# A vision-transformer tower on one core: the small steps of each image rebuilt and put in other places of the attention loop

## The reference

```python
emb = jnp.einsum('bnk,ek->bne', patches, W) + b            # embed
h = emb + pos_embed
...
q = (x @ Wq + bq).reshape(B, N, H, hd)                     # x = _layernorm(h)
k = (x @ Wk + bk).reshape(B, N, H, hd)
v = (x @ Wv + bv).reshape(B, N, H, hd)
scores = jnp.einsum('bihd,bjhd->bhij', q, k) / jnp.sqrt(jnp.asarray(hd, x.dtype))
...
attn = jax.nn.softmax(scores + col_bias[None, :, None, :], axis=-1)
out = jnp.einsum('bhij,bjhd->bihd', attn, v).reshape(B, N, D)
h = h + (out @ Wo + bo)
...
logits = tokens.astype(jnp.float32) @ router_w.astype(jnp.float32).T   # tokens = _layernorm(h)
combine = jnp.zeros((N, E), tokens.dtype).at[jnp.arange(N)[:, None], re].set(rw)
for e in range(E):
    g = jax.nn.gelu(tokens @ w1[e] + b1[e], approximate=False)
    out = out + combine[:, e:e + 1] * (g @ w2[e] + b2[e])
```

## Time and profile before

| | |
|---|---|
| median of 3 executions | 1240.35 us (1239.73 to 1240.62) |
| profiled execution, its own time | 1236.63 us |
| its span, first to last instruction | 1234.4 us |
| PE busy | 1131.5 us (92%) |
| ACT busy | 1034.6 us (84%) |
| DVE busy | 737.2 us (60%) |
| POOL busy | 117.8 us (10%) |
| start, until the first exponential | 73.7 us |
| attention, first to last exponential | from 73.70 to 1071.66 us |
| granted PE clock, each of 40 slices | 9 tenths or more (mean 1.000) |

### The profile page before, as it was taken

One profiled execution on the slowest core, in us unless ns is written; L12 is line 12 of the kernel. 1 busy time (PEld: TensorE's weight loads), 2 busy tenths in 40 slices (PEclk: granted clock), 3 DMA queues, 4 the chain that ended last, 5 costly groups with the idle time before them and its releaser, 6 DMA issues. The chain is left out here.

```text
span 1234.4 us, 23587 instructions
## 1 busy us (share of the span) xinstructions
PE 1131.5 (92%) x8738; PEld 343.7 (28%) x8738; DVE 737.2 (60%) x1953; ACT 1034.6 (84%) x1124; POOL 117.8 (10%) x128
## 2 busy tenths in 40 slices
PE   2269999999999999999999999999999999899998
PEld 2022222222222222222222222222222222243332
DVE  8734365656565656565657575757565641567654
ACT  0059999999999999999999999999999999945553
POOL 4303010101010101000101000000000100000000
PEclk9999999999999999999999999999999999999999
DMA  1133131323131313131313132222222230022231
GB/s 39 53 79 82 37 84 45 81 49 81 49 80 50 80 50 80 49 80 50 80 51 79 50 77 53 68 55 77 59 66 57 58 85 4 14 64 69 65 85 48
DMA packets 61672, 75.96 MB, mean 62 GB/s; under 512 B 25988, under 2 KB 31108, under 8 KB 61532
## 3 DMA queue, kind: packets, MB, share of 16 engines
q1 hardware_dynamic: 59452, 73.78, 23.3%
q10 hardware_dynamic: 1600, 0.27, 0.1%
q0 software_dynamic: 480, 0.06, 0.1%
HBM read 37.47 MB, written 36.49 MB: 60 GB/s over the span
## 5 line engine op out<-in xcount | busy, mean ns | idle before, releaser
L1126 ACT ACTIVATE probs<-psum 128x1024 f32<-128x1024 f32 x1024 | 951.2, 1106 | 46.1 <-PE psum L1319 45.4
L1335 PE MATMUL psum<-probs,VA 128*32 128x512 f32 x4096 | 545.6, 605 | 8.2 <-DVE oT L1194 7.4
L1319 PE MATMUL psum<-QA,KA 54*128 54x512 bf16 x2048 | 349.4, 386 | 34.0 <-ACTq L1145 10.3
L1319 PEld LDWEIGHTS psum<-QA,KA 54*128 54x128 bf16 x2048 | 81.5, 93 | 535.7 <-ACT probs L1126 493.2
L1335 PEld LDWEIGHTS psum<-probs,VA 128*32 128x32 f32 x4096 | 82.6, 108 | 139.2 <-issue 105.1
L1194 DVE STREAM_TRANSPOSE oT<-psum 128x512 f32<-128x512 f32 x64 | 45.8, 715 | 122.9 <-PE psum L1335 122.2
L1161 ACT ACTIVATE probs<-psum,b 128x1024 f32<-128x1024 f32 x64 | 67.8, 1110 | 54.3 <-PE psum L1388 54.2
L1266 DVE TENSOR_TENSOR probs<-probs,psum 128x1024 f32<-128x1024 f32 x64 | 78.1, 1221 | 51.6 <-PE psum L1398 32.5
L1126 ACT ACT_TABLE_LOAD x1 | 1.3, 1283 | 72.4 <-issue 72.4
L1388 PE MATMUL psum<-m_x,w 64*128 64x512 f32 x256 | 60.5, 591 | 1.5 <-ACT probs L1161 1.5
L1412 PE MATMUL psum<-probs,w 128*64 128x512 f32 x256 | 60.9, 598 | 0.0
(11 more groups left out here) (182 smaller groups left out, 936.8 us busy)
## 6 DMA issues: line engine op xcount, KB each, us to landing
QA<-q_parts_d SPq DMA_DIRECT2D x64, 192.0 KB
KA<-k_parts_d SPq DMA_DIRECT2D x64, 192.0 KB
q_parts_d<-qk_parts SPq DMA_DIRECT2D x32, 192.0 KB, 2.5
k_parts_d<-qk_parts SPq DMA_DIRECT2D x32, 192.0 KB, 2.7
xT<-in_xT SPq DMA_DIRECT2D x16, 256.0 KB, 3.4
q_parts_d<-qk_parts SPq DMA_DIRECT2D x32, 128.0 KB, 2.7
k_parts_d<-qk_parts SPq DMA_DIRECT2D x32, 128.0 KB, 2.5
x_d<-x2T SPq DMA_DIRECT2D x16, 256.0 KB, 2.0
```

Source lines behind the costliest of these rows:

```text
L1126: nc.scalar.activation(probs[:, k % PROB_BUFS, :], score_buf(buf_of(k)), ACT.Exp).then_inc(exped, 1)
L1319: last = pe.matmul(score_buf(buf_of(k))[:, (g % 2) * BANK:(g % 2 + 1) * BANK], KA[rows_of(h, SCORE_ROWS), h // 2, jt * P:(jt + 1) * P], QA ...
L1335: last = pe.matmul(o_acc[32 * g:32 * g + 32, :], VA[:, jt, h, :], probs[:, k % PROB_BUFS, (g % 2) * BANK:(g % 2 + 1) * BANK], start=(jt == ...
```

## The change

1. **Block-diagonal weights.** The weights of `embed`, `v` and `out_proj` are laid out as 128 x 128 with the 64 x 64 matrix twice on the diagonal. The tokens of an image's first and second half stand above each other on the partitions, so one matmul gives two chunks of tokens. Eight matmuls with 64 columns become four with 128.
2. **fp32 instead of three bf16 parts.** The normalised tokens are transposed in fp32 (`norm_t`, four transposes, as in `post_t`) and projected in fp32. `split_tokens`, `norm_t0` and `norm_t1`, the splitting of the weights on POOL at the start, and the three-turn matmuls go. `qk0` and `qk1` are each two fp32 matmuls with 64 rows and 256 columns.
3. **Halves.** `qk0`, `qk1`, `out_proj`, `router`, `v` and `embed` are each issued in two halves in two slots. With the five steps that stay whole there are 17 pieces. Only the second half raises `aux_filled`.
4. **Another order.** See the table in the diff. `qk1` instead of `v` is now followed by the splitting of q and k. `evacuate` now stands ahead of the slot's step in DVE's queue. `centre_tokens` moves from behind `out_proj` to slot 9 and `scale_tokens` to slot 10, both ahead of the read-out of `sq`. The ranking moves to slots 20 and 22, and the router's exponential on ACT from block 52 to block 39.
5. **Two images ahead.** `embed` and `norm_t` work for the image after the next. The start therefore embeds two images (`FIRST_STEPS`), and SP loads patches three images ahead.
6. **The output bias.** It was a row of `w_o` fed by a row of ones in `oT_norm`. Now POOL adds it to the residual once for each image (`add_bo`, 128 x 512 fp32), and DVE waits for that before `out_proj` is read out. Because of the new layout of `w_o` one second transposition of `evacuate` (`ON`) serves all, at slot 1, instead of two.

```diff
-AUX_SLOTS = {2: ["embed"], 7: ["norm_t0"], 8: ["norm_t1"], 9: ["qk0"], 10: ["qk1"], 11: ["v"], 14: ["sq"],
-             18: ["out_proj"], 19: ["flag"], 23: ["post_t"], 25: ["router"], 31: ["combine_t"]}
+AUX_SLOTS = {0: ("qk0", 0), 1: ("qk0", 1), 3: ("qk1", 0), 4: ("qk1", 1), 6: ("out_proj", 0), 7: ("out_proj", 1),
+             10: ("sq", 0), 13: ("post_t", 0), 15: ("flag", 0), 16: ("router", 0), 18: ("router", 1), 20: ("v", 0),
+             21: ("v", 1), 23: ("embed", 0), 24: ("embed", 1), 26: ("combine_t", 0), 29: ("norm_t", 0)}
+FIRST_STEPS = [("embed", 0), ("norm_t", 0), ("qk0", 0), ("qk1", 0), ("v", 0), ("embed", 1), ("norm_t", 1), ("sq", 0),
+               ("flag", 0)]
+CENTRE_SLOT, SCALE_SLOT, NORM_SLOT = 9, 10, 27
-COMBINE_SLOT = 26
+COMBINE_SLOT, WEIGH_SLOT = 20, 22
...
+            def add_bo(b):
+                g.wait_ge(xn_made, b + 1)
+                rows = H_all[:, ds(b * NCH, NCH), :]
+                g.tensor_tensor(rows, rows, b_o[:, :].unsqueeze(1).broadcast_to([P, NCH, D]),
+                                ALU.add).then_inc(bo_added, 1)
...
                 if step == "embed":
                     pe.wait_ge(x_loaded, 16 * (n + 1))
-                    for c in range(NCH):
-                        last = pe.matmul(aux[:, c * D:(c + 1) * D], xT[:, c * P:(c + 1) * P], w_tok[:, :],
+                    for c in chunks:
+                        last = pe.matmul(aux[:, c * P:(c + 1) * P], xT[:, c * P:(c + 1) * P],
+                                         w_tok[:, :, :].rearrange("k t e -> k (t e)"), start=True, stop=True)
...
+                elif step in ("qk0", "qk1"):
+                    rows = slice(D * int(step[-1]), D * int(step[-1]) + D)
+                    for i in halves:
+                        cols = slice(i * BANK // 2, (i + 1) * BANK // 2)
+                        last = pe.matmul(aux[:, cols], w_qk[rows, :, :].rearrange("k a e -> k (a e)"), xnT[rows, cols],
                                          start=True, stop=True)
...
+                def body(b):
+                    add_bo(b)
+                    if b:
+                        post_pow(b - 1)
...
+                        if slot == LAST_EVAC_SLOT and b:
+                            evacuate(b - 1, 3)
+                        if slot in EVAC_SLOTS:
+                            evacuate(b, EVAC_SLOTS[slot])
+                        if slot == CENTRE_SLOT and b:
+                            centre_tokens(b - 1, st)
+                        if slot == SCALE_SLOT and b:
+                            scale_tokens(b - 1, st)
+                        if slot == NORM_SLOT and b + 2 < NB:
+                            normalise(b + 2)
+                        found = step_of(b, slot)
+                        if found and is_last(found[0], found[1]):
```

More of the change, by code:

```diff
@@ L69, with step_of, is_last, aux_order @@
 TINY = 1e-30
-QK_COLS, V_COLS = slice(0, 2 * D), slice(2 * D, 3 * D)
-W_COLS = 3 * D
-TURNS = ((0, 0), (1, 0), (2, 1))
 SECOND = 64
 Q_ROWS = SECOND + H
-ONE_ROW = 31
 ds = bass.ds
 FB_UNITS = 4 * NCH
[L85 to L97, removed]
+def step_of(b, slot):
+    if slot not in AUX_SLOTS:
+        return None
+    step, part = AUX_SLOTS[slot]
+    image = b + (2 if step in LEAD else 1 if step in PREP else -1)
+    return (step, part, image) if 0 <= image < NB else None
+def is_last(step, part):
+    return part == 1 or step not in HALVED
+def aux_order(b):
+    found = [step_of(b, slot) for slot in range(QUADS)]
+    return [f[0] for f in found if f and is_last(f[0], f[1])]
+def aux_before(b):
+    return len(FIRST_STEPS) + sum(len(aux_order(i)) for i in range(b))
+def aux_count(b, step):
+    return aux_before(b) + aux_order(b).index(step) + 1
 def token_unit(b):
@@ L572, in tensor_steps, with aux_step @@
         def tensor_steps(pe):
-            def aux_step(step, n, done, drained):
-                pe.wait_ge(aux_drained, drained) if not (isinstance(drained, int) and drained == 0) else None
+            def aux_step(step, n, drained, part=None):
+                halves = (0, 1) if part is None else (part,)
+                chunks = [c for c in range(NCH // 2) if c // 2 in halves]
+                if drained and 0 in halves:
+                    pe.wait_ge(aux_drained, drained)
                 if step == "embed":
@@ L634, in aux_step @@
                                             ident_bf[:, :])
-                last.then_inc(aux_filled, 1)
+                if 1 in halves or step not in HALVED:
+                    last.then_inc(aux_filled, 1)
             return aux_step
@@ new lines, in _ @@
+                    link(v.memset(lower[:, :, :], 0.0))
+                    for e in range(1, NX):
+                        last = v.memset(lower[:, e, 0:e], 1.0)
+                    last.then_inc(const_ready, 1)
+                    v.wait_ge(w_loaded, 16 * WEIGHTS)
+                    for i, (step, n) in enumerate(FIRST_STEPS[1:7]):
+                        if step in LEAD:
+                            lead_step(step, n, i + 2)
+                        else:
+                            prep_step(step, n, i + 2, st)
+                        if step == "embed":
+                            normalise(n)
@@ L1145, in fallback, with body @@
                         act.sem_inc(fb_moved, FB_MOVED)
-                def body(b, first, last):
+                def body(b):
                     act.wait_ge(flag_ready, b + 1)
@@ L1153, in body @@
                         exp_block(b, k)
-                        if k == ROUTER_EXP_BLOCK and not first:
-                            router_exp(aux_base(b) + aux_order(not last, True).index("router") + 1)
+                        if k == ROUTER_EXP_BLOCK and b:
+                            router_exp(aux_count(b, "router"))
                 def gelu(u):
```

361 lines of the change are left out of this document (169 added, 192 removed).

## The result

The kernel after takes 1314.06 us (median of 5, 1307.64 to 1316.02) against 1240.35: 1.0586 of the time, 95% interval 1.0569 to 1.0603. It is slower, as forecast, but by 74 us and not by 35: outside the range of 1247 to 1298. The profiled execution took 1307.64 us (before: 1236.63), with a span of 1305.6 and a mean granted PE clock of 0.967 (before: 1.000).

The account below looks back on a forecast made before the run. ACT was taken as the bound, idle only when PE's scores come late. 1236.6 + 30 (attention) + 5 (start) - 0.9 (experts) + 1 (POOL) = 1271.7 profiled; with 3.7 to the median, 1275 us; range 1247 to 1298.

Parts of the forecast that it names:

- The bound: Attention, kernel before: ACT bounds, idle 2.8 us an image waiting for PE's scores; 58.8 us if PE were never late.
- the 0.78: Between scores and `values`: PE may be 0.78 us late before ACT loses any time.
- the ledger: PE's lateness per quad: falls 0.30, rises by step times and waits, excess over 0.78 lost; 6.05 us an image.
- Slots 13 to 16: PE waits for DVE's read-outs ahead of `post_t` and `flag`, then half of `router`: 3.15 us an image lost.
- Slots 0 to 4: Halves of `qk0` and `qk1`, with PE waiting for `oT` and `qk0`'s read-out: 1.45 us an image lost.
- Slot 26: `values` waits for `oT` behind DVE's normalisation of `embed`: 0.85 us an image lost.
- The pieces: PE time of new halves: 0.57 us for `embed`, `v`, `out_proj`, 0.54 for `qk`, 0.5 for `router`; all under 0.78.
- POOL's addition: `add_bo` at an image's start, some 2.3 us long: costs 0.1 us an image, +1 us in all.
- The rival with the shared port: `oT_norm` waits for `add_bo` to end, up to 1.5 us an image: 1297 us; chance 0.10.
- The start: Before the first exponential: 8.2 us of second `embed` on DVE less 3.0 saved, +5 us (bounds +3 and +7).
- The experts: Expert stretch: `out_proj` has half as many instructions, -0.9 us.
- the price of the wait ahead of `flag`: Slot 15: PE waits 2.3 us for `post_t`'s read-out, losing 1.85 us an image.

Follow-up runs that it names:

- d: kernel 1 with POOL's `add_bo` moved from the image's start to behind `prep_rstd`: 62.63 us an image against 63.02, 1237.22 us.
- b: kernel 1 with DVE reading `qk0` out ahead of `evacuate` in slot 1: 61.85 us an image against 63.02, 1227.12 us.
- experiment 6: The kernel after with all DVE and POOL reorderings, every step whole in its second half's slot: 1203.38 us, against 1200.08 with halves.
- kernel 1: The kernel after with DVE's work on `sq` that follows `excess` moved behind the read-out of `flag`: 1243.08 us, 63.02 us an image.
- kernel 1 with five additions: kernel 1 with five idle 512-column additions on DVE ahead of the read-out of `post_t`: 1303.29 us, 67.8 us an image.

## Why the prediction was right, and where it was wrong

- **The bound, the 0.78 and the ledger** held. Full-clock images took 64.98 against 64.8.
- **Slots 13 to 16** (3.15 forecast): waits of 1.21 and 2.12 against 1.2 to 1.4 and 2.3. Taken away they gave back 0.99 and 1.96.
- **Slots 0 to 4** (1.45): `qk1` waited 0.92, not 0.75. Without POOL's addition it waits 0.5 (d), so DVE's own chain was 0.25 shorter than forecast and the addition gave 0.4 of the wait. b gave back 1.17.
- **Slot 26** (0.85): 0.87.
- **The pieces**: a half 0.64 where I took 0.57, within the bounds; `qk` 0.52 where I took 0.54 (475.61 to 476.13). Little hangs on it, as experiment 6 shows.
- **POOL's addition**: 1.29 us long, not 2.3, and dearer than I took it: 0.39 an image, 6 us and not 1. The rival with the shared port had the place right, and about a quarter of its price of 1.5 us an image was measured.
- **The start**: +2.45, not +5. DVE was later at the bias by 59.64 - 54.42 = 5.2 us, as the working said, and the shift rows were as late. But before, their 24 KB went out at 65.53 and the load that waits for them was issued at 70.29 (4.8 us), behind the loads of the parts, issued from 62.42 to 65.4; after, it took from 70.70 to 72.74. That the loads ahead of them make the difference is read from the order alone. A wait ended last that the sum didn't look for: the transfers'.
- **The experts**: -1.0 against -0.9.

Profiled execution against profiled execution, the sum was 1271.7 and the time 1307.64, so 35.9 are missing, and the clock is 36. That these meet so well is partly luck: the start came 2.5 us cheaper than forecast, and the attention at full clock dearer (33 against 31 + 1 in thirteen images, +0.4 against -1.3 in the other three, the last of which had a fall too). **The step that failed is the price of the wait ahead of `flag`**, 1.85 us an image in the sum: "PE waits 2.3" was right, and the price was taken as if PE came back from the wait at the same speed. At full clock it was worth 1.96; the fall of the granted clock to 0.50 behind it added 3.1 in most images. In the kernel before, `values` after an `evacuate` was PE's only place of waiting for DVE in the attention, for 0.5 us at most, as its table of waits has it:

```profile
PE psum L1335 <- DVE oT L1194: 7.4, 17, 0.5
```

So no row of it could show what one of 2.3 does, and in its profiled execution the granted clock never fell in that stretch. But a wait over four times as long as any that was read is an operation without a row, and the sum gave what it may bring neither a rival nor a place in the range. Each rival ran at full clock, so the range of 1247 to 1298 held full-clock times alone. The rest of the way to the median, 1314.06, goes with the clock too: it was 0.960 to 0.963 in the other executions, of which there is no trace.

## What to carry to other kernels

In an alternating chain between two engines, read for each step what stands in the reader's queue ahead of its read-out. Here other places for four blocks in DVE's queue and one in POOL's, and one step of PE a slot later, with every instruction kept, turned +5.9% into -3%, while cutting the steps in halves gave 0.3%. And where a change makes TensorE wait some us in each round, price the wait twice, once at its length and once with the work behind it at the lower clock, and keep both in the range.

## What the runs showed of the hardware

- At a wait of 1.9 to 2.4 us of an otherwise busy PE, the granted clock fell to 0.50 in 12 of 14 images (in each of three kernels: 1.9, 2.1 and 2.35 us), and `values` took 1.93 us instead of 1.06. At 1.3 us it fell in one image of 14, at 0.7 in none. The same place and nearly the same wait can go either way.
- The clock stayed down for 3.4 or 6.8 us in most cases, once each for 10.2 and 17.1. An image of the kernel after, and of kernel 1 with five additions, lost some 0.45 us for each us of it (1.5, 3.1, 4.6 and 7.8), one of the kernel before 0.37.
- A DVE product of two SBUF tiles took 0.70 us instead of 0.29 beside a POOL addition of two SBUF tiles.
- Eight fp32 matmul instructions of 128 columns in a row held PE 1.09 us, two groups of four 0.64 each.
